# Attention kernel: the value matmuls of a unit in seven blocks in place of eight

## What is computed

```python
q = (x @ Wq.T).reshape(b, t, h_kv, g, d).transpose(0, 2, 3, 1, 4)   # 8 kv heads, g = 4 query heads each, d = 32
k = (x @ Wk.T).reshape(b, t, h_kv, d).transpose(0, 2, 1, 3)
v = (x @ Wv.T).reshape(b, t, h_kv, d).transpose(0, 2, 1, 3)
att = jnp.einsum('bhgqd,bhkd->bhgqk', q, k) / scale
att = jax.nn.softmax(att, axis=-1)
y = jnp.einsum('bhgqk,bhkd->bhgqd', att, v)
```

## Time and profile before

| what | value |
|---|---|
| median of three executions | 3395.23 us (3391.97 to 3398.03) |
| profiled execution, its own time | 3392.18 us |
| span of the profile | 3390.5 us |
| granted TensorE clock over the span | 0.997 of full |
| TensorE busy | 3343.5 us, 99% of the span |
| attention, one unit from unit 9 on | 49.5 us |

### The profile page before, as it was taken

How to read it: one execution, slowest core, us unless ns; L and a number is a source line. 1 busy time by engine, 2 the same in 40 slices (tenths; PEclk the granted TensorE clock), 3 DMA queues, 4 the chain that set the end, 5 groups by cost and what they waited for, 6 DMA issues and landing times.

```text
span 3390.5 us, 45326 instructions
## 1 busy us (share of the span) xinstructions
PE 3343.5 (99%) x16999; PEld 2311.3 (68%) x16999; DVE 2252.6 (66%) x3764; ACT 1584.8 (47%) x2992; POOL 1616.3 (48%) x726
## 2 busy tenths in 40 slices
PE   7999999999999999999999999999999999999999
PEld 5788555555555555555555478888888888887887
DVE  5766887788788778878877398544444444444728
ACT  3211576766666666666666633222112222124544
POOL 1223789999999999999999700000000000001010
PEclk9999999999999999999999999999999999999999
DMA  7567655656565565656555645511111111004222
GB/s 242 193 206 214 168 108 115 125 108 126 109 131 116 110 127 110 124 110 132 112 112 122 160 158 179 152 28 30 31 31 31 31 30 31 25 31 141 97 72 90
DMA packets 197620, 370.35 MB, mean 109 GB/s; under 512 B 44288, under 2 KB 119552, under 8 KB 179008
## 3 DMA queue, kind: packets, MB, share of 16 engines
q0 software_dynamic: 39808, 204.24, 26.2%
q1 hardware_dynamic: 154176, 157.45, 16.4%
q10 hardware_dynamic: 3456, 6.29, 0.6%
HBM read 168.29 MB, written 64.87 MB: 69 GB/s over the span
## 4 chain that ended last, share of the span: by engine, by line
PE 89%; DVE 5%; DMA 3%; ACT 1%; issue 1%; POOL 0%; SPq 0%; ACTq 0%; DVEq 0%; POOLq 0%
PE att_scores L1189 15%; PE att_scores_T L1203 14%; PE att_y_acc L1214 14%; PE gu_gate_acc L1790 14%; PE gu_up_acc L1790 13%; PE down_acc L2123 4%; PE wo_acc L1483 4%; PE qkv_qk_acc L629 3%; PE att_den_acc L907 2%; PE down_acc L2154 2%; DMA qkv_wqkv_raw<-in_wmod 1%; DMA qkv_wmod_lo<-in_wmod 1%; ACT qkv_h_affine L346 1%; PE qkv_v_acc L610 1%; DVE qkv_wmod L462 1%
## 5 line engine op out<-in xcount | busy, mean ns | idle before, releaser
L1116 DVE TENSOR_REDUCE att_chunk_max<-att_scores 128x1 f32<-128x512 f32 x1984 | 1211.4, 680 | 292.2 <-PE att_scores L1189 292.2
L1084 ACT ACTIVATE att_exp<-att_scores_T 128x512 f32<-128x512 f32 x2032 | 1030.6, 624 | 401.6 <-PE att_scores_T L1203 394.5
L1017 POOL TENSOR_TENSOR att_exp_pair<-att_exp 128x2048 f32<-128x2048 f32 x252 | 1180.4, 4759 | 69.7 <-ACT att_exp L1084 67.8
L1214 PE MATMUL att_y_acc<-att_exp,att_v_head 128*32 128x512 f32 x4096 | 492.7, 598 | 0.5 <-ACT att_exp L1084 0.5
L1647 POOL DMA_DIRECT2D inter_scratch<-gu_inter x84 | 45.2, 538 | 853.7 <-DVE gu_inter L1524 853.7
L1189 PE MATMUL att_scores<-att_kq,att_q_stack 96*128 96x512 f32 x768 | 315.2, 416 | 0.5 <-DVE qkv_qk_out_lo L442 0.3
L1189 PE MATMUL att_scores<-att_k_stack,att_q_stack 96*128 96x512 f32 x768 | 315.6, 414 | 0.2 <-DMA att_q_stack<-att_max_T_lo 0.2
L1203 PE MATMUL att_scores_T<-att_q_stack,att_kq 98*128 98x512 f32 x768 | 301.5, 400 | 0.0
L1203 PE MATMUL att_scores_T<-att_q_stack,att_k_stack 98*128 98x512 f32 x752 | 295.5, 405 | 0.7 <-ACT att_exp L1084 0.7
L1712 ACT ACTIVATE gu_magnitude<-gu_value 128x512 f32<-128x512 f32 (+1 forms) x88 | 55.7, 633 | 511.6 <-DVE gu_value L1748 511.6
L1214 PEld LDWEIGHTS att_y_acc<-att_exp,att_v_head 128*32 128x32 f32 x4096 | 106.7, 109 | 234.0 <-ACT att_exp L1084 144.4
(11 more groups left out here) (250 smaller groups left out, 6064.1 us busy)
## 6 DMA issues: line engine op xcount, KB each, us to landing
att_exp_pair<-att_exp_pair POOLq DMA_DIRECT2D x128, 1024.0 KB, 7.4
att_q_stack<-q_scratch SPq DMA_DIRECT2D x72, 256.0 KB, 5.6
qkv_wqkv_raw<-in_wmod POOLq DMA_DIRECT2D x32, 512.0 KB, 4.4
shared_raw<-in_wd_t POOLq DMA_DIRECT2D x34, 256.0 KB, 2.9
qkv_x_tile<-in_x SPq DMA_DIRECT2D x16, 512.0 KB, 4.0
q_scratch<-qkv_qk_out_hi POOLq DMA_DIRECT2D x32, 256.0 KB, 3.8
q_scratch<-qkv_qk_out_lo POOLq DMA_DIRECT2D x32, 256.0 KB, 4.3
y_scratch<-att_y_out SPq DMA_DIRECT2D x32, 256.0 KB, 2.7
```

Of the source, the lines that this page charges most:

```text
L1017: nc.gpsimd.tensor_tensor(ps[PAIR_SLOT[j]][:], pr[2 * j % NP][:], pr[(2 * j + 1) % NP][:], ALU.add).then_inc(pair_done, 1)
L1084: nc.scalar.activation(pr[k % NP][:, h * NB:(h + 1) * NB], st_bank(u, GH * k + h)[:], ACT.Exp, scale=INV_SQRT_DH).then_inc(exp_done, 1)
L1116: nc.vector.reduce_max(cmax[c % 2][:, q:q + 1], turn_buffer(u, q)[:], AX.X).then_inc(sm_done, 1)
L1214: ins = nc.tensor.matmul(yp[h * DH:(h + 1) * DH, :], vg[c // QB % 2][:, k, :], pr[k % NP][:, h * NB:(h + 1) * NB], start=(k == 0), stop=(k ...
```

## The change

The steps at which values are issued, and the tiles in each block, are now written in a table. Steps 0, 2, 4 and 6 stay as they were. Then tiles 6, 7 and 8 go at step 9, tiles 9, 10 and 11 at step 12, and tiles 12 and 13 at step 14; tiles 14 and 15 go at the next unit's step 0, as before. Steps 8 and 10 have no block. S comes before T at steps 9, 12 and 14 too.

```diff
--- before.py
+++ after.py
@@ -674,6 +674,8 @@
     DMA_AFTER = {1: 0, 3: 1, 4: 2, 7: 3}
     LATE_DMA_AFTER = {1: 0, 3: 1, 5: 2, 7: 3}
     EARLY_MAX = 14
+    VALUES_AT = {0: (-2, -1), 2: (0, 1), 4: (2, 3), 6: (4, 5), 9: (6, 7, 8), 12: (9, 10, 11), 14: (12, 13)}
+    SCORE_FIRST = (4, 6, 9, 12, 14)
     QUAD_AFTER = 5
     DEN_SLOT = (0, 4, 3)
     ND = len(DEN_SLOT)
@@ -1226,12 +1228,12 @@
                     if k == 0:
                         pe.wait_ge(m_stored, 32 + u * 32)
                     transposing = not beyond(u, 1) and k == transpose_step(u)
-                    if k % 2:
+                    if k not in VALUES_AT:
                         for h in range(GH):
                             ahead_turn()
                             scores_t(u, c, k, h)
                         continue
-                    spare = not is_first(u) and k not in DEN_AT[1:]
+                    spare = not is_first(u) and k not in SCORE_FIRST
                     for h in range(GH - 1):
                         if not spare:
                             scores_t(u, c, k, h)
@@ -1243,11 +1245,11 @@
                             ahead_turn()
                         if spare:
                             scores_t(u, c, k, h)
-                    for b in (2, 1):
-                        if k > 0:
-                            by_v(u, c, g, k - b)
+                    for j in VALUES_AT[k]:
+                        if j >= 0:
+                            by_v(u, c, g, j)
                         elif not is_first(u):
-                            by_v(u - 1, (c - 1) % BODY, g, KT - b)
+                            by_v(u - 1, (c - 1) % BODY, g, KT + j)
                     if k in DEN_AT and not is_first(u):
                         denominators(pe, u - 1, DEN_AT.index(k))
                     ahead_turn()
```

## The result

The changed kernel takes 3402.56 us (median of 20 runs, 3400.05 to 3407.27), the kernel before 3396.73 beside it on the same chips (20 runs, 3390.80 to 3399.39). The ratio is 1.0022, with a 95% interval of 1.0016 to 1.0028. The kernel became slower, by 5.8 us; the interval leaves out 1 and lies on both sides of the 0.2% that the prediction took as the least that can be told. Forecast were 3.9 us and 3399.1 us, in a range of 3388 to 3409. Of the 3.5 us between 3399.1 and 3402.56, 1.5 is the median of the kernel before, which is 3395.23 in the three executions shown and 3396.73 in the twenty.

A forecast was written before the change was run, and what follows sets the result against it. TensorE was taken as the bound, busy 99% of the span. The terms 0 + 1.5 + 0.1 + 1.2 + 0 + 1.1 made 3.9 us more, a median of 3399.1 us, in a range of 3388 to 3409.

The forecast's parts named there:

- the middle of the kernel: Units 9 to 29, steps 6 to 14: 8.70 + 8.74 + 6.88 = 24.32 us, against 24.32 before, so nothing.
- the last unit: Unit 31: ScalarE sets the pace, load_y is issued 1.1 us later, and the term costs 1.1 us.
- the block's own cost: Each value block costs TensorE about 0.34 us for being a block; one less in 32 units gives 10.9 us.
- Two long stretches: Steps 6 to 9 and 9 to 12: twelve T and S on end wait for PSUM banks; intervals 8.70 and 8.74 us.
- Wait before step 9: Steps 6 to 9: S12 waits for exponential 9, the block starts at 5.99, 0.18 us of waiting.
- Wait before step 12: Steps 9 to 12: X waits for a maximum delayed 0.26 by the row maximum; interval 8.74 us.
- S first at step 14: Steps 12 to 14: the ninth T comes last and waits for nothing; 0.16 us comes back, interval 6.88.
- Units 0, 1 to 7 and 8: Early units, steps 6 to 14: 26.59, 24.53 and 24.83 us, costing 1.2, 1.5 in all and 0.1.
- Only the switch counts: Rival: the long stretches' waits don't come, each of units 9 to 29 saves 0.52 us; 3382 us, chance 0.13.
- Three banks: Rival: T12 and X have three banks in turn, wait 0.5 and 0.6 more in 30 units; 3432 us, chance 0.05.
- Pair sums: Rival: pair sum 4's 0.9 us delay passes through GpSimd's chain in each unit; 3427 us, chance 0.07.
- Everything behind it moves: Last unit, SyncE's queue: row loads, y of unit 30 and gate and bias loads follow load_y, 1.1 us later.

The follow-up runs named there:

- experiments 5: The kernel before with maxima and exponentials over half of the columns, so the output is not attention's: 3373.97 us, one run.
- experiment 6: The changed kernel with maxima and exponentials over half of the columns, so the output is not attention's: 3366.33 us, one run.
- experiment 8: The changed kernel with exponentials over half of the columns and whole maxima, output not attention's: 3390.50 us, one run.
- experiment 10: The kernel before with S first in blocks where nine T stand, and also at the odd step after X: 3388.84 us, ratio 0.9979.
- experiment 1: The changed kernel with the last unit's table and order as before, units 0 to 30 still changed: 3398.07 us, ratio 1.0011.
- experiment 2: The kernel before with the new table and order in the last unit alone: 3398.77 us, ratio 1.0011.
- experiment 4: The kernel before with the last unit alone changed, and GpSimd's third DMA sum there also waiting for tiles 10 and 11: 3394.67 us, ratio 1.0000.
- experiment 3: The changed kernel with T first again at steps 9, 12 and 14, so the table alone: 3415.21 us, ratio 1.0065.
- Experiment 9: The kernel before, its table kept, with S first only in the blocks before which nine T stand: 3392.50 us, ratio 0.9991.
- experiments 5 to 8: The kernels with half reads; number 7 is the changed kernel with half-column maxima and whole exponentials, output not attention's: 3393.65 us, one run.

## Why the prediction came out as it did

**The whole.** 3.9 us were forecast and 5.8 measured, with the middle of the kernel at nothing for the reasons given and one term, the last unit, far too small. That the sum of the middle came out so exactly is luck in part.

**What bounds the kernel, and the block's own cost: right.** A block less is worth 0.34 a unit where nothing waits; experiments 5 and 6 give 0.36. The Trainium skill, TensorEngine Tiling (Array Packing), Key Properties, says that a change of tiling mode drains the engine. The 0.36 is in keeping with it, but no run here sets the draining apart from anything else that a block brings.

**Two long stretches: right in kind, one size off.** Wait before step 9: forecast 0.18, measured 0.20. Wait before step 12: forecast 0.34 (8.74), measured 0.24 (8.64). I let X run 0.16 behind its release, as I had for a T. The rows above show 0.06, for X as for a T on which TensorE has waited. A T pays the other 0.1 at the S behind it, which comes 0.34 on in place of 0.23; so the formula gave today's 4.33 by two errors that cancel, and it failed for X, which has the block behind it. The delay by the row maximum, 0.26, was right. The Trainium skill, TensorEngine Tiling (Array Packing), PSUM Bottleneck, says that PSUM copies may become the bottleneck once tiling has sped TensorE up. It agrees with these rows in so far as emptying the banks is what a stretch of twelve waits for: faster readers give 0.55 a unit back.

**S first at step 14: right in kind, one size off.** 6.98, forecast 6.88. The ninth T no longer waits, but 0.1 is lost to ScalarE (6.89 in units 9 to 29 of experiment 8, where the exponentials are fast). That it is the pair of T behind X, which I did not follow to ScalarE, is shown on the kernel before by experiment 10; in the changed kernel the order is the same, but it was not tried. The two sizes cancel by luck: 24.34 against 24.32.

**Units 0, 1 to 7 and 8: right.** 26.58, 24.56 and 24.83, forecast 26.59, 24.53 and 24.83. In unit 3 one interval was 9.22 and not 8.7, with VectorE waiting 1.85 us at the reciprocal for the denominators' DMA. Such single long intervals are in unit 3 or 4 of every trace, before's too (0.3 us in unit 4, and 0.9 there in experiment 1), so this one is not the change's. Experiment 1 puts the whole of these units at 0.11% (0.02 to 0.20), where the sum had 2.8 us, 0.08%.

**The rivals.** Only the switch counts: wrong, by the rows at 8.72 and 8.64, and it is what experiment 6 looks like. Three banks: wrong, 9.2 does not occur in units 9 to 29. Pair sums: the 0.9 came as forecast (0.96), and the 1.22 of idle took it.

**The last unit: the term that was too small.** "Everything behind it moves" by 1.1 took `load_y`'s delay as the cost. The delay came (1.2 in experiment 2), and nothing behind it moved by that; the row loads did not move at all. What I passed over is that SyncE's queue and GpSimd's are two, and that `load_y` stood only 1.0 ahead of a 1 MB sum in the other. A delay of 1.1 turned the order round, the load took 9.7 us or more instead of 6.3, and ScalarE's copy, which had no wait at all before, came 3.6 to 4.5 late. The unit's own stretch from step 6 to 14 also grew by 0.7, which the sum didn't have. That unit costs 0.11% by experiment 2 instead of the 0.03% of the sum, and experiment 4 takes it away by moving the one DMA. With 3.7 in place of 1.1 the sum is 6.5 us, 0.19%; the interval of the result is 0.16 to 0.28%. So the middle of the kernel came out at nothing, as forecast, and the side on which the result fell was decided by the last unit.

**What stays open.** How much of the cost in the medians is the lower clock near the end of attention. A stretch at 0.50 that no long wait of TensorE came before is in the traces of the changed kernel and of experiments 3, 4 and 9, but not in those of before and of experiments 1 and 10 (in experiment 2 it came behind its wait). Experiment 9 has before's order in the last unit, and its stretch lies in unit 30, so the change isn't needed for it. The kernels with half reads, experiments 5 to 8, have low stretches near the end of attention too. Over all executions the mean granted clock is 0.9948 for the changed kernel, 0.9951 in experiment 2, 0.9954 in experiment 4, 0.9959 in experiment 1 and 0.9958 for before beside experiments 1 and 2. But the clock isn't all: of the executions at 0.996, the changed kernel's take 3401.1 on average (3 of them), experiment 2's 3396.5 (5), experiment 4's 3394.3 (3) and before's 3394.4 (12). No experiment set the clock apart from the waits beside it.

## What to carry to other kernels

Merging blocks on an engine that bounds the kernel gives back their fixed cost only as far as the readers of its outputs are ahead: count the longer stretch against the pace of each reader and the number of banks, and the gain may be nil before it is tried. The order of the two products around such a place can be worth more than the number of blocks; give the slower release the last place in the stretch, and let no two of one kind stand in a row. When a step delays a DMA, look not only at who waits for it but at which large transfer on any other queue it now falls behind, or comes close to.

## What the runs showed of the hardware

- A load of 512 KB landed after 4.1 us when issued 2.58 us ahead of an accumulating DMA of 1 MB on another queue (experiment 4), after 6.1 to 6.3 when 0.7 to 1.0 ahead (before, experiments 1 and 9), and after 9.7 to 10.5 when 0.2 to 0.5 behind it (experiments 2 and 3, the changed kernel). The one issued next to it landed after 12.4 when 0.30 ahead (experiment 1).
- TensorE's granted clock fell to 0.50 (1.2 GHz) in stretches of the last unit of the changed kernel's trace where it was not idle but issued one S for each exponential: nine matmuls in the 4 us before. A three-tile block took 4.16 instead of 2.71 there. It also fell after the idle 4.5 us. In before's trace the same pace in that unit went on at full clock (20.72 us at 1.00).
- When TensorE has waited for a maximum, the weights and the matmul that take its bank both start 0.05 to 0.06 us behind its end, with 16 columns of weights (X) as with 128 (T). An S behind such a T comes 0.33 to 0.34 on and not 0.234 (before at 1290.24, experiment 3 at 1285.06).
